# Keys turned in 32x32 blocks on VectorE and by DMA in place of TensorE transposes, and a new order of TensorE's work in a slot

## The reference

```python
qkv = silu(xn @ w_qkv.T)                       # q, k, v: 128 features each, per head
o_intra = ((q @ k.T) * diag_decay) @ v         # inside a block
o_inter = (q * q_decay) @ kv                   # with the state of all blocks before
kv      = block_decay * kv + (k * k_decay).T @ v
out     = norm_w * rms_normalise(o_intra + o_inter)
return (sigmoid(xn @ w_gate.T) * out) @ w_out.T
```

## Time and profile before

| | |
|---|---|
| median of 3 runs | 1833.52 us (1833.5 to 1834.05) |
| the profiled execution | 1832.82 us, its span 1831.1 us |
| PE busy, of the span | 1793.9 us, 98% |
| PE weight loads | 1605.3 us, 88% |
| DVE busy | 1169.4 us, 64% |
| ACT busy | 760.4 us, 42% |
| mean DMA traffic | 109 GB/s |

### The profile page before, as it was taken

The page is one execution under the profiler, slowest core; times in us unless marked ns, Lnnn a source line. Parts: engine busy times, 40 slices in busy tenths (PEclk is TensorE's granted clock), DMA queues, the critical chain, the costliest instruction groups (busy, mean ns, idle before and its releaser), DMA issues.

```text
span 1831.1 us, 34221 instructions
## 1 busy us (share of the span) xinstructions
PE 1793.9 (98%) x12597; PEld 1605.3 (88%) x12597; DVE 1169.4 (64%) x2367; ACT 760.4 (42%) x1427; POOL 320.6 (18%) x314
## 2 busy tenths in 40 slices
PE   6999999999999999999999999999999999999998
PEld 5888899999888888888888888889999999999997
DVE  7888777777454544544545445467777777765565
ACT  4333334333444544544445445443333333433331
POOL 2232345545000000000000000023232323200011
PEclk9999999999999999999999999999999999999998
DMA  6655422323344444444444444422121213200013
GB/s 220 220 207 213 141 90 81 108 66 102 98 138 123 122 138 123 121 137 123 136 124 123 139 120 123 139 85 81 59 87 53 90 58 94 72 31 1 1 58 104
DMA packets 174900, 199.00 MB, mean 109 GB/s; under 512 B 19600, under 2 KB 154256, under 8 KB 174736
## 3 DMA queue, kind: packets, MB, share of 16 engines
q1 hardware_dynamic: 150032, 138.09, 24.8%
q0 software_dynamic: 12288, 33.57, 5.7%
q10 hardware_dynamic: 12416, 25.17, 3.7%
HBM read 110.76 MB, written 86.00 MB: 107 GB/s over the span
## 4 chain that ended last, share of the span: by engine, by line
PE 93%; DVE 4%; issue 1%; ACT 1%; DMA 0%; SPq 0%; DVEq 0%; ACTq 0%
PE bank L1139 7%; PE bank L1119 7%; PE bank L1141 7%; PE bank L1140 7%; PE bank L1121 6%; PE bank L1120 6%; PE bank L1163 6%; PE bank L1180 6%; PE bank L1171 6%; PE bank L1183 6%; PE bank L1210 5%; PE bank L1218 3%; PE bank L1192 3%; PE bank L1194 3%; PE bank L1193 3%; PE bank L1156 3%
## 5 line engine op out<-in xcount | busy, mean ns | idle before, releaser
L1139 PE MATMUL bank<-wh,xh 128*128 128x256 f32 x1024 | 311.0, 304 | 0.0
L503 POOL DMA_INDIRECT yk<-slot_y,pos x128 | 125.8, 983 | 1011.4 <-DMA slot_y<-ys 748.8
L1141 PE MATMUL bank<-wh,xl 128*128 128x256 f32 x1024 | 288.8, 282 | 0.0
L1140 PE MATMUL bank<-wl,xh 128*128 128x256 f32 x1024 | 288.3, 282 | 0.0
L588 ACT ACTIVATE kv<-bank 128x512 f32<-128x512 f32 x256 | 152.9, 597 | 300.2 <-PE bank L1141 300.2
L940 DVE SCALAR_TENSOR_TENSOR state<-state,hc,bank 128x128 f32<-128x128 f32 x448 | 155.8, 348 | 86.6 <-PE bank L1171 73.1
L1139 PEld LDWEIGHTS bank<-wh,xh 128*128 128x128 f32 x1024 | 193.6, 189 | 15.9 <-issue 15.9
L1119 PE MATMUL bank<-xh,wh 128*128 128x512 f32 x512 | 207.2, 405 | 0.0
L1121 PE MATMUL bank<-xh,wl 128*128 128x512 f32 x512 | 202.4, 395 | 0.0
L1120 PE MATMUL bank<-xl,wh 128*128 128x512 f32 x512 | 202.0, 395 | 0.0
L1140 PEld LDWEIGHTS bank<-wl,xh 128*128 128x128 f32 x1024 | 193.8, 189 | 0.0
(11 more groups left out here) (162 smaller groups left out, 3600.2 us busy)
## 6 DMA issues: line engine op xcount, KB each, us to landing
slot_x<-zeros ACTq DMA_DIRECT2D x8, 3072.0 KB, 10.2
we<-wexp_in SPq DMA_DIRECT2D x192, 128.0 KB, 2.3
xs<-slot_x SPq DMA_DIRECT2D x96, 256.0 KB, 2.7
slot_y<-ys SPq DMA_DIRECT2D x96, 256.0 KB, 2.4
wd<-wdown_in SPq DMA_DIRECT2D x192, 64.0 KB, 2.2
raw<-wqkv_in SPq DMA_DIRECT2D x16, 384.0 KB, 3.7
xin<-x_rows SPq DMA_DIRECT2D x8, 512.0 KB, 4.4
xn_rows<-xn SPq DMA_DIRECT2D x8, 512.0 KB, 5.5
```

Of the source, the lines that this page charges most:

```text
L1139: pe.matmul(dst, lh, rh, start=(k == 0), stop=False)
L1140: pe.matmul(dst, lh, rl, start=False, stop=False)
L1141: mm = pe.matmul(dst, ll, rh, start=False, stop=(k == KD - 1))
```

## The change

Three things change.

1. The keys' transposes on PE and their copy on ACT go. DVE's new `turn_keys` turns each 32x32 block of the keys in one instruction and writes `kz` (its innermost index, c, is the chunk); SP stores `kz` to DRAM and loads it back in four DMAs of 32 partitions each, which brings each block to its partitions in `kT`.
2. `kT` has the chunk as its innermost index, so the weights of chunk c are read with a step of four f32 elements (16 bytes) from one column to the next.
3. PE's order in a slot: both halves of `project_kv` stand first, `keys_values` comes before `gate_up`, and `scores(s-1)` stands behind `project_out(s-2, 0)`, right ahead of `down(q0)` and `project_q`. SP's program is written as one loop over slots, with the keys' transfers in it.

```diff
-        kT = keep("kT", [P, SB])
+        kz = keep("kz", [P, BLK, TB, CH])
+        kT = keep("kT", [P, BLK, TB, CH])
@@ SP
+            def store_keys(i):
+                sp.wait_ge(kz_ready, i + 1)
+                sp.dma_start(kz_dram[i % 2], kz[:].rearrange("p b j c -> p b (j c)")).then_inc(kz_stored, 16)
+
+            def load_keys(i):
+                sp.wait_ge(kz_stored, 16 * (i + 1))
+                sp.wait_ge(s_mm, i)
+                for b in range(BLK):
+                    sp.dma_start(kT[b * TB:(b + 1) * TB, :, :, :].rearrange("p a j c -> p a (j c)"),
+                                 kz_back[i % 2, b]).then_inc(kT_loaded, 16)
...
+            for s in range(SLOTS + 1):
+                q0 = 2 * (s - EXPERT0)
+                if EXPERT0 < s <= EXPERT1:
+                    pair_done(q0 - 1)
+                if s > FIRST_OUT + 3:
+                    store_last(s - FIRST_OUT - 4)
+                if s < NSTEP:
+                    store_keys(s)
+                if s in COMBINE:
+                    store_part(COMBINE.index(s))
+                if s < NSTEP:
+                    load_keys(s)
+                if 4 <= s < ROUTE0 + 3 * NSB and s % 3 == 1:
+                    load_rows_to_scatter(s // 3)
+                if s == EXPERT0 - 1:
+                    first_pairs()
+                if EXPERT0 <= s < EXPERT1:
+                    pair_done(q0)
...
@@ ACT
-            def copy_kT(i):
-                act.wait_ge(kT_mm, i + 1)
-                act.copy(kT[:], bank[2][:]).then_inc(kT_ready, 1)
@@ DVE
+            def turn_keys(i):
+                dve.wait_ge(k_silu, i + 1)
+                dve.wait_ge(v_silu, i + 1)
+                dve.wait_ge(kz_stored, 16 * i)
+                dve.transpose(kz[:].rearrange("p b j c -> p b c j"), kv[i % 2][:, :, 0:HD].rearrange("p c (b i) -> p b c i", i=TB)).then_inc(kz_ready, 1)
...
+                if projects:
+                    turn_keys(s)
                 if attends:
                     decay_scores(s - 1)
@@ PE
-            def turn_keys(i):
-                pe.wait_ge(sm_ready, i)
-                pe.wait_ge(mask_ready, NSB)
-                for c in range(CH):
-                    mm = pe.transpose(bank[2][:, ch[c]], kv[i % 2][:, c, 0:HD], ident[:])
-                mm.then_inc(kT_mm, 1)
...
-                    mm = pe.matmul(bank[2][:, ch[c]], kT[:, ch[c]], qT[:, ch[c]], start=True, stop=True)
+                    mm = pe.matmul(bank[2][:, ch[c]], kT[:, :, :, c].rearrange("p a j -> p (a j)"), qT[:, ch[c]], start=True, stop=True)
```

More of the change, by code:

```diff
@@ L48 @@
 assert len(COMBINE) == NT
-HEAD_BEFORE_ROWS = {2: 2, 5: 3, 7: 4}
+TB = 32
+BLK = P // TB
 def updates_before(i, c):
@@ L246, in lightning_moe @@
         q_mm = sem("q_mm")
-        kT_mm = sem("kT_mm")
+        kz_ready = sem("kz_ready")
+        kz_stored = sem("kz_stored")
         g_mm = sem("g_mm")
@@ L255, in lightning_moe @@
         q_silu = sem("q_silu")
-        kT_ready = sem("kT_ready")
+        kT_loaded = sem("kT_loaded")
         tanh_done = sem("tanh_done")
@@ L375, in _, with load_rows_to_scatter @@
                 group(g)
[L377 to L381, removed]
+            def store_keys(i):
[7 more added lines that the diff above has]
+                                 kz_back[i % 2, b]).then_inc(kT_loaded, 16)
+            def load_rows_to_scatter(q):
                 for r in range(CH):
@@ L394, in load_experts, with first_pairs, pair_done @@
                     sp.dma_start(wd[r][j * F:(j + 1) * F, :], at(wdown, e)).then_inc(pair_loaded[r], 16)
[L396 to L413, removed]
+            def first_pairs():
+                sp.wait_ge(routed, 1)
+                sp.wait_ge(wgt_ready, 1)
+                for q in range(2):
+                    load_experts(q)
+                for r in range(CH):
+                    sp.wait_ge(scattered[r], 16 * TOPK * NT // CH)
+                for q in range(2):
+                    load_rows(q)
+            def pair_done(q):
+                sp.wait_ge(y_mm, q + 1)
+                if q + 2 < NPAIR:
+                    load_rows(q + 2)
+                    load_experts(q + 2)
+                sp.wait_ge(ys_ready, q + 1)
+                sp.dma_start(slot_y_pair[q], ys[q % 2][:]).then_inc(y_stored[q % 2], 16)
             def load_part(t):
@@ L417, in load_part, with store_part @@
                 sp.dma_start(xr[t % 2][:], part_tile[t]).then_inc(xr_loaded[t % 2], 16)
[L419 to L423, removed]
-                if s in COMBINE:
[L425 to L429, removed]
+            def store_part(t):
+                sp.wait_ge(summed, TOPK * (t + 1))
+                sp.dma_start(part2_tile[t], xr[t % 2][:]).then_inc(part2_stored[t % 2], 16)
@@ new lines, in load_last, with store_last @@
+            def load_last(b):
+                if b < 2:
+                    for r in range(2):
+                        sp.wait_ge(part2_stored[r], 16 * NT // 2)
+                else:
+                    sp.wait_ge(out_stored[b % 2], 16 * (b // 2))
+                sp.dma_start(res[b % 2][:], part2_grp[b]).then_inc(res_loaded[b % 2], 16)
+            def store_last(b):
+                sp.wait_ge(final, CH * (b + 1))
+                sp.dma_start(out_grp[b], res[b % 2][:]).then_inc(out_stored[b % 2], 16)
@@ new lines, in _ @@
+            sp.wait_ge(xn_stored, 16 * NSB)
+            next_head(1)
+            load_rows_to_scatter(0)
+            for s in range(SLOTS + 1):
[6 more added lines that the diff above has]
+                    store_keys(s)
+                if s in COMBINE:
+                    store_part(COMBINE.index(s))
[7 more added lines that the diff above has]
+                    pair_done(q0)
+                if s == EXPERT1:
+                    for r in range(2):
+                        sp.wait_ge(y_stored[r], 16 * NPAIR // 2)
+                    for t in range(2):
+                        load_part(t)
+                if s in COMBINE and COMBINE.index(s) + 2 < NT:
+                    load_part(COMBINE.index(s) + 2)
@@ L430, in _ @@
                 if s % NSB == 5 and s // NSB + 2 < NH:
                     next_head(s // NSB + 2)
[L433 to L442, removed]
+                if s == FIRST_OUT:
+                    for b in range(2):
+                        load_last(b)
@@ L443, in _ @@
+                if FIRST_OUT + 4 <= s < FIRST_OUT + 2 + NSB:
+                    load_last(s - FIRST_OUT - 2)
             for r in range(2):
@@ L1256, in _ @@
                     project_kv(s, 0)
-                if attends:
-                    scores(s - 1)
+                    project_kv(s, 1)
                 if experts:
@@ L1262, in _ @@
                     turn_back(s - FIRST_OUT - 3)
[L1263 to L1266, removed]
                 if s == 0:
@@ L1272, in _ @@
                     keys_values(s - 1)
+                if experts:
+                    gate_up(q0)
                 if delivers:
                     project_out(s - 2, 0)
+                if attends:
+                    scores(s - 1)
                 if experts:
```

11 lines of the change are left out of this document (6 added, 5 removed).

## The result

The changed kernel takes **2011.78 us** (median of 4 runs, 2010.58 to 2017.65); the kernel before took 1833.51 (4 runs, 1833.44 to 1834.05) beside it. The ratio is 1.0977, its 95% interval 1.0964 to 1.099. The prediction was 1952 us in a range that ends at 1980: the sign is right, and 60 us are missing. Times of e1 to e8 and e12 are single runs; the kernel before spread by 10 us in 13 runs beside e9 to e12, and by 3 us in 9 runs beside e13 and e14.

A forecast was written before the change was run, and what follows sets the result against it. PE's own instructions, one after another, were taken as the bound. From the profiled 1832.8 us: -56 transposes, +70 stall, +95 step, +3 DVE, +4 and +3 ends gave 1951.8, with 0.7 to the median 1952 us; range 1842 to 1980.

The forecast's parts named there:

- The transposes: On PE's chain: removing four transposes a slot saves 0.44 us in each of 128 slots, -56 us.
- The stall: Expert slots: PE waits ahead of down(q0) for DVE's hT, about 1.45 us in each of 48 slots, +70 us.
- T+1.68: Expert slots: when down(q0)'s load can start, with T the start of the scores' last pass.
- The other 80 slots: Slots without experts: project_q covers sm, so attend does not wait, with 0.5 us to spare.
- The step: Scores' weight loads on PE: the 16-byte step costs 93 ns a load over 1024 loads, +95 us.
- the bound of 7/8: Scores' loads: if each slot's first load hides under the long matmul ahead, only 7/8 of the step's price shows.
- DVE's instruction: DVE's new turn_keys takes 0.9 us, covered in expert slots; +3 us in routing, combining and weight-splitting slots together.
- The way through DRAM: Keys' store and loads: about 7 us from turning to kT in place, 10 us available, so hidden.
- Ends: turn(0) in slot 26 waits for rows behind slot 25's keys, +4 us; last_sum in the last slots, +3 us.
- The free step: Rival for the scores' weight loads: the 16-byte step costs nothing, 1857 us in all; chance 0.30.
- SP's queue as the bound: Rival for expert slots: the store lands in 5.5 us, SP needs 18.0 us a slot, 1995 us; chance 0.08.
- Faster: Rival: free step, and 53 us of gaps ahead of loads around down vanish in the wait, 1804 us; chance 0.07.

The follow-up runs named there:

- e1: Kernel before, old order and PE transposes kept; ACT's copy leaves kT interleaved, so the scores' weights have a 16-byte step: 2043.37 us (kernel before 1940.78).
- e8: Changed kernel with ACT copying the keys into a contiguous kT, and DVE's order add_out(s-2, 0), gated, decay_scores: 1896.81 us (kernel before 1833.3).
- e12: e6 with the scores back where they stood in the kernel before, ahead of turn(q0): 2004.26 us (kernel before 1936.87).
- e9: e6 with DVE's order turn_keys, gated, add_out(s-2, 0), decay_scores: 1977.29 us, ratio 1.0206 to the kernel before.
- e13: e9 with the first two expert pairs issued before slot 25's keys, and load_keys(s) after the first pair in expert slots: 1799.17 us, ratio 0.9812.
- e14: e9 once more, on the same chip as e13: 1855.74 us, ratio 1.0111 to the kernel before.
- e5: Kernel before, its transposes and contiguous kT kept, with PE's new order alone: 1933.54 us (kernel before 1833.3).
- e6: Changed kernel with contiguous kT, so no step in the weights, and DMA pieces of 128 bytes: 1896.57 us (kernel before 1833.3).
- e3: Changed kernel with gated(q0) ahead of decay_scores(s-1) on DVE: 2013.63 us (kernel before 1940.78).
- e11: e5 with DVE's order of e9, PE's transposes kept: 1943.67 us, ratio 1.0037 to the kernel before.
- e4: Changed kernel with add_out(s-2, 0) moved from behind decay_keys to directly behind turn_keys on DVE: 2087.11 us (kernel before 1940.78).
- e2: Kernel before with kT laid out so that the scores' weights are read with a step of 8 bytes: 1945.16 us (kernel before 1940.78).
- e7: Changed kernel with ACT copying the keys that DMA brought with a step into a contiguous kT: 1925.03 us (kernel before 1833.3).

## Why the prediction was right and wrong

e5 and e6 split the 178 us: the order +100.2, the other way of turning -37.0, the step +115 (2011.78 - 1896.57; the kernel before was at 1833.5 and 1833.3 in the two). The prediction had +73, -49 and +95 for these, and the three differences of 27, 12 and 20 are the 60 us that were missing. e5 and e6 are one run each, but none of the three differences is as small as the 3 us by which the kernel before spread on a quiet chip.

- **The transposes, -56: right, but not kept whole.** e6 against e5 gives -0.39 us in a slot of 74 to 121 and -0.45 in one of 27 to 73, e13 -0.43 and -0.21. Of 56 us, e6 keeps 37: against e5 it loses 5.4 ahead of slot 2 (the first scores) and 5.9 ahead of slot 26 (`turn(0)`).
- **The stall, +70: right in place, cause, count and size.** 48 waits for `hT`, gone when `gated` goes first (e3). From the scores' last pass to `down` are 1.70 us in e5, where T+1.68 was forecast, and 0.205 where nothing is waited for (e9, e11, e13): 1.50 each, 72 us. The changed kernel has 970.39 - 968.59 = 1.80; `sm` starts 0.42 after the last pass instead of 0.31, since that pass is 0.38 long now, and that is part of the step's price. A slot of 27 to 73 is 1.63 longer in e5; the 0.14 over stays when the stall is gone (e11), some 7 us for which the prediction had no term.
- **The other 80 slots, "no wait there": the step that failed.** `attend` indeed did not wait. But DVE's later instructions were not followed one further: behind `sm` and the states stands the `acc` that empties the bank of `project_out`. e5 puts that at 14.4 + 4.5 + 2.2 = 21 us, and from the last pass of `attend` to L1229 it has 26.7 us in 79 places where 3.3 had been: 23 us; only 3 (last_sum) had been allowed. How it is made was shown by e4 and by e13, in which it is gone. With 72 for the stall and 7 for the order itself these are 102 us, against the +100 of e5.
- **The step, +95: mechanism right, size a little small, and the clock left out.** A load that shows costs 0.121 us, more than DVE's 93 ns and than the upper bound of 0.11; but only seven of the eight in a slot show, as the bound of 7/8 had it: 0.85 a slot, 109 us. e6 has it at 0.87 in a median slot of 27 to 73 and 0.81 in one of 74 to 121. The prediction counted all of PE's prices at the upper clock, and this failed: in slots 27 to 73 the changed kernel has eight falls, e6 none, and they are some 12 of the 115 us.
- **The skill's rule.** The Trainium skill, "SBUF — State Buffer" (Door 1: The DMA port swizzle), has four fp32 stepped over for free. Here 16 bytes, exactly four fp32, cost a load of 327 ns against 191 (e1), and 8 bytes next to nothing (e2: 201): the half of that note which asks for two hits in a line of 16 bytes agrees with the runs, the other does not.
- **DVE's instruction, 0.9 us: near.** It takes 1.105. The surcharge for the step was right (0.39 us from e6's 0.711 to 1.105, where 0.37 was said); the base was not, since a contiguous transposition takes 0.71 and not the 0.50 of `kp`. It is never on the path of an expert slot, as said.
- **The way through DRAM, hidden: right but for the first scores**, which wait 4.8 us. I had counted the ten us from a slot of the steady state, and from `keys_values` to the first scores are only 5.8 us.
- **Ends.** `turn(0)` waits 6.30 us instead of 2.49, +3.8 where +4 stood; but in this wait, and in that of the first scores, the clock falls for 6.8 us and is still low when PE goes on, which the prediction had not counted.

```profile
505.25 1.09 PE L1240 MATMUL bank<-ident,xs 128*128 128x128 f32 x4 [6.30 <-issue]
```

- **The rivals.** The free step fell with e1. SP's queue as the bound (8%) was wrong for this kernel, whose slots had become 17.3 us long, and right for the kernel behind it: e9 and e14 sit on it at 16.1. The price was a store that lands in about 3 us, as measured, not 5.5. "Faster" fell for this kernel; 1799 us were reached by another one, with the layout, DVE's order and SP's order changed together, and not in the way that the rival named.
- **The range.** Its lower end adds up to 1845 us from its own terms, not 1842; this changes no reading.

In slots 27 to 73 the clock falls eight times where stall and step are both there (after, e4), in the same slots but for two, and never with the step alone (e1, e3) or the stall alone (e5 to e8). So in these kernels it took both. Why these eight of 47 slots stays open, and so do the one or two falls of e9, e12 and e14, where PE waits for `turn`'s rows.

## What to carry to other kernels

Where an instruction is moved back in one engine's order, follow everything behind its consumer on the next engine, down to the last buffer that is given back, not only the first hand-over: here that was 21 us in slots declared free of waits. A layout that interleaves so that the DMA gets longer pieces is paid for in every later access, here on PE's loads seven times a slot; measure 16-byte steps before use, 8-byte ones are harmless here. And a queue that waits for its own store should have other work put between the two; here that was worth 51 us in slots 27 to 73 (754.7 to 704.1), once PE no longer hid it.

## What was not expected of the hardware

- A step of 16 bytes between fp32 elements slows each engine's access, written or read: PE's load of 128 columns 191 to 324 ns (pass to pass 0.112 to 0.233 us), ACT's copy of 512 columns 581 to 1091 when it writes them so (e1) and 1104 when it reads them so (e7), DVE's transposition 711 to 1105. A step of 8 bytes costs 201 ns on the load and 621 on the copy.
- With pieces of 128 bytes the 256 KB store of keys lets its loads go 3.5 us after its issue (e9), with 2 KB after at most 2.0 (967.03 to 969.05 in the changed kernel, where they also waited for the scores). It shows only where SP's queue is the bound. The rows of the changed kernel's queue:

```profile
967.03 0.33 SPq L385 DMA_DIRECT2D keys_turned<-kz  x1
969.05 1.74 SPq L391 DMA_DIRECT2D kT<-keys_turned  x4
```

- PE's granted clock fell to its lower level for some 3.4 us behind a stop of 1.4 us, in 8 of 47 slots that all have this stop, and in none of them when its loads were the fast ones (e5 to e8). In the stops of 4.8 and 6.3 us it fell for 6.8 us.
